# Early safe rows, later result loads, another order at the end of the attention and the choice in five units: attention and expert layers on one Trainium2 core

## What is computed

```
x = x + attn_a(layernorm(x))   # 16 heads, latent 32, rotary positions, causal softmax
x = x + ffn(layernorm(x))
x = x + attn_b(layernorm(x))   # 16 heads of 8, causal softmax
x = x + ffn(layernorm(x))

def ffn(flat):                 # 4096 x 128
    logits = flat @ gate_w + gate_b                  # 8 experts
    topv, topi = top_k(logits, 2); topw = softmax(topv)
    return sum over e of (gelu(flat @ w1[e] + b1[e]) @ w2[e] + b2[e]) * weight of e
```

## Time and profile before

| | us |
|---|---|
| median of three runs | 1233.25 |
| lowest and highest | 1228.84, 1236.98 |
| profiled execution, its own time | 1235.08 |
| its span | 1233.3 |
| mean granted TensorE clock | 0.918 |
| PE, DVE, ACT, POOL busy | 1038.6, 860.1, 656.8, 734.7 |

### The profile page before, as it was taken

One profiled execution on the slowest core, in us unless ns is written; L12 is line 12 of the kernel. 1 busy time (PEld: TensorE's weight loads), 2 busy tenths in 40 slices (PEclk: granted clock), 3 DMA queues, 4 the chain that ended last, 5 costly groups with the idle time before them and its releaser, 6 DMA issues.

```text
span 1233.3 us, 31859 instructions
## 1 busy us (share of the span) xinstructions
PE 1038.6 (84%) x11223; PEld 779.5 (63%) x11224; DVE 860.1 (70%) x2217; ACT 656.8 (53%) x1205; POOL 734.7 (60%) x809
## 2 busy tenths in 40 slices
PE   4689999988888988449988888999999974499995
PEld 3466666666665656239988745666666642398995
DVE  4697889888789997525565577677777764255665
ACT  1266776656465655115544556777777741154552
POOL 0476776767667777715544424667878866155553
PEclk9699999889699999769999989999999987599998
DMA  5340000000000000222333200000000002223335
GB/s 118 82 87 3 2 2 2 11 10 10 8 10 12 11 10 19 74 55 72 96 93 92 82 18 1 2 2 10 15 17 14 19 20 70 52 76 98 101 104 147
DMA packets 69358, 53.27 MB, mean 43 GB/s; under 512 B 20770, under 2 KB 61346, under 8 KB 69218
## 3 DMA queue, kind: packets, MB, share of 16 engines
q1 hardware_dynamic: 56578, 29.78, 9.6%
q0 software_dynamic: 9088, 18.70, 4.6%
q10 hardware_dynamic: 3552, 2.95, 1.0%
HBM read 27.57 MB, written 23.81 MB: 42 GB/s over the span
## 4 chain that ended last, share of the span: by engine, by line
PE 50%; DVE 25%; issue 8%; SPq 7%; DMA 4%; POOL 3%; ACT 2%; DVEq 0%; POOLq 0%; ACTq 0%
PE PS L1851 7%; PE PS L1533 5%; PE PS L1612 5%; PE PS L1663 4%; PE PS L1535 4%; PE PS L1534 4%; PE PS L1594 3%; DMA xg<-expert_in 3%; DVE M L1004 3%; DVE swapped L1032 2%; DVE M L996 2%; PE PS L1601 2%; SPq L582 2%; PE PS L1643 2%; DVE swapped L1030 2%
## 5 line engine op out<-in xcount | busy, mean ns | idle before, releaser
L1310 ACT ACTIVATE PT<-PS 128x768 f32<-128x768 f32 x256 | 206.7, 808 | 118.0 <-PE PS L1680 69.9
L754 POOL DMA_INDIRECT expert_out<-y_rows,dest x156 | 151.9, 974 | 194.8 <-DVE y_rows L1224 170.3
L643 POOL TENSOR_SCALAR_AFFINE_SELECT PT<-PT 128x512 f32<-128x512 f32 x256 | 185.7, 726 | 85.2 <-ACT PT L1310 84.4
L1446 ACT ACTIVATE hid<-PS,b_cols 128x256 f32<-128x256 f32 x312 | 122.2, 474 | 93.9 <-PE PS L1535 93.9
L1851 PE MATMUL PS<-W,hid 128*128 x1248 | 152.3, 275 | 0.2
L660 POOL DMA_INDIRECT expert_in<-rows,slots x128 | 130.0, 1015 | 29.6 <-issue 25.0
L1851 PEld LDWEIGHTS PS<-W,hid 128*128 128x128 f32 x1248 | 146.2, 192 | 0.5 <-issue 0.5
L1612 PE MATMUL PS<-PT,v_aug 128*32 128x256 f32 (+1 forms) x2048 | 115.1, 345 | 2.5 <-POOL PT L643 2.5
L1594 PE MATMUL PS<-causal_b,ident_b 128*128 128x256 bf16 x512 | 103.8, 287 | 8.2 <-DVE q_aug L1096 7.2
L1533 PE MATMUL PS<-xg_hi,w_hi 128*128 128x256 f32 x312 | 96.4, 309 | 2.3 <-DVE xg_lo L1203 1.7
L683 POOL TENSOR_TENSOR straight<-whole,C 128x512 f32<-128x512 f32 x64 | 82.8, 1293 | 21.0 <-ACT whole L1329 19.9
(11 more groups left out here) (292 smaller groups left out, 3159.9 us busy)
## 6 DMA issues: line engine op xcount, KB each, us to landing
xg<-expert_in SPq DMA_DIRECT2D x78, 129.0 KB
got<-expert_out SPq DMA_DIRECT2D x64, 128.0 KB
expert_out<-y_rows,dest POOLq DMA_INDIRECT x156
W<-in_L_ffn_w_dram SPq DMA_DIRECT2D x1, 2048.0 KB, 10.4
expert_in<-rows,slots POOLq DMA_INDIRECT x128
expert_in<-C SPq DMA_DIRECT2D x16, 128.0 KB
out_dram<-X SPq DMA_DIRECT2D x8, 256.0 KB
b_rows<-in_L_ffn_b_dram SPq DMA_DIRECT2D x2, 512.0 KB
```

What stands on the lines that cost most here:

```text
L643: nc.gpsimd.affine_select(out=diagonal, in_=diagonal, pattern=[[0, 4], [1, P]], compare_op=ALU.is_ge, fill=0.0, base=0, channel_multiplier ...
L754: nc.gpsimd.indirect_dma_start(out=expert_out, out_offset=bass.IndirectOffsetOnAxis(ap=dest[:, i % 4, b_:b_ + 1], axis=0), in_=y_rows[:, i ...
L1310: s.activation(PT[:, unit % 2, 2 * pair:2 * pair + 2, 0:3 * P], PS[:, 4:6, 0:3 * P], ACT.Exp).then_inc(m["exp_done"], 1)
L1446: ins = s.activation(hid[:, r % 2, k, :], h_bank[r % 2][k // 2][:, k % 2 * ROWS:(k % 2 + 1) * ROWS], ACT.Gelu, bias=b1_cols[:, bass.ds(e * ...
```

## The change

- `KNOWN` = 4 and `SAFE` = 3 x 512 + 256 = 1792. The ends are taken from the counts of chunk 4, as soon as its rank is done (in unit 1 of chunk 7's cycle in attention A, unit 0 in B), and 1792 rows behind each end are filled: up to 3 x 512 tokens may still come, and a tile may reach 256 rows further. The fills stand in SP's queue ahead of the wait for the attention's end; rows go out before numbers. The constant `aside` and `expert_out` grow with it.
- POOL waits for all fills before it sends chunk 5 (`send`, at k = 0), since the sends of chunks 5 to 7 overwrite safe rows.
- SP issues each result load one slot later than before; ACT waits for `attended` in place of `ends_ready`.
- `LAST`: out_t and out of chunk 7 come ahead of gate_t and gate of chunk 6; the statistics of chunk 7 use the other of two buffers, so that they don't meet those of chunk 6.
- In attention A POOL does the second `mask` of a unit in the next unit, behind `end_rope`, and the send behind `start_rope`.
- `PARTS_A`: the 13 parts of the choice stand in units 3 to 7, two, three, three, three and two of them, in place of units 4 to 7 with four, three, two and four.

```diff
+KNOWN = NCH - 4
+SAFE = (NCH - 1 - KNOWN) * CH + ROWS
...
-    put("aside", 2 * T + p[:, None] + P * np.arange((2 * E - 1) * RB))
+    put("aside", 2 * T + p[:, None] + P * np.arange((E * SAFE + SPARE) // P))
...
-    LAST = [("rank", 0, -2, 4), ("turn", 1, 0, 7), ("gate_t", 0, -1, 0), ("gate", 0, -1, 1), ("out_t", 0, 0, 2), ("out", 0, 0, 3), ("rank", 0, -1, 4),
+    LAST = [("rank", 0, -2, 4), ("turn", 1, 0, 7), ("out_t", 0, 0, 2), ("out", 0, 0, 3), ("gate_t", 0, -1, 0), ("gate", 0, -1, 1), ("rank", 0, -1, 4),
...
-PARTS_A = {4: range(0, 4), 5: range(4, 7), 6: range(7, 9), 7: range(9, 13)}
+PARTS_A = {3: range(0, 2), 4: range(2, 5), 5: range(5, 8), 6: range(8, 11), 7: range(11, 13)}
...
             for n, e_ in (("a", "1"), ("b", "2")):
                 me = moe_sems[e_]
-
-                sp.wait_ge(attended[n], 1)
-                sp.dma_start(b2_rows[:, :, :]...).then_inc(me["bias_ready"], 16)
 
                 sp.wait_ge(me["ends_ready"], 1)
                     for e in range(E):
-                        end = sp.value_load(end_of[0:1, e:e + 1], min_val=0, max_val=E * STRIDE - ROWS)
-                        sp.dma_start(expert_in[bass.ds(end, ROWS), D:WIDE].rearrange("(j p) w -> p j w", p=P),
-                                     con("aside")[:, e * RB:(e + 1) * RB].unsqueeze(2)).then_inc(me["filled"], 16)
-                        sp.dma_start(expert_in[bass.ds(end, ROWS), 0:D].rearrange("(j p) w -> p j w", p=P),
-                                     ident.unsqueeze(1).broadcast_to([P, RB, D])).then_inc(me["filled"], 16)
+                        end = sp.value_load(end_of[0:1, e:e + 1], min_val=0, max_val=E * STRIDE - SAFE)
+                        sp.dma_start(expert_in[bass.ds(end, SAFE), 0:D].rearrange("(j p) w -> p j w", p=P),
+                                     ident.unsqueeze(1).broadcast_to([P, SAFE // P, D])).then_inc(me["filled"], 16)
+                        sp.dma_start(expert_in[bass.ds(end, SAFE), D:WIDE].rearrange("(j p) w -> p j w", p=P),
+                                     con("aside")[:, e * SAFE // P:(e + 1) * SAFE // P].unsqueeze(2)).then_inc(me["filled"], 16)
+
+                sp.wait_ge(attended[n], 1)
+                sp.dma_start(b2_rows[:, :, :]...).then_inc(me["bias_ready"], 16)
...
                     load(i, r, least)
-                    if least >= LAG:
-                        load_results(i - LAG, (least - LAG) % CT, least - LAG)
+                    if least > LAG:
+                        load_results(i - LAG - 1, (least - LAG - 1) % CT, least - LAG - 1)
...
-                for tok in range(first_late, first_late + CT):
+                for tok in range(first_late - 1, first_late + CT):
...
                         pool.wait_ge(m["targets_ready"], c + 1)
+                        if c == KNOWN + 1:
+                            pool.wait_ge(moe_sems["1" if n == "a" else "2"]["filled"], 16 * 2 * E)
...
                     if unit and plan.project[unit - 1]:
                         end_rope(plan.project[unit - 1])
+                    if unit:
+                        mask(m, unit - 1, 1)
                     mask(m, unit, 0)
+                    if plan.project[unit]:
+                        start_rope(plan.project[unit])
                     if sends_at(unit, FIRST_SENT["a"]):
                         chunk, k = sends_at(unit, FIRST_SENT["a"])
                         send("a", chunk, range(k, k + 1))
-                    if plan.project[unit]:
-                        start_rope(plan.project[unit])
-                    mask(m, unit, 1)
...
+            def known_ends(m, me, s):
+                if s.c == KNOWN:
+                    dve.wait_ge(m["freed_dve"], s.freed)
+                    v.tensor_copy(end_of[:, :], counts[0:1, KNOWN, :]).then_inc(me["ends_ready"], 1)
...
-                own.did(v.tensor_copy(end_of[:, :], counts[0:1, NCH - 1, :]))
...
-                v.memset(scratch1[:, :], 0.0).then_inc(m["ends_ready"], 1)
...
-                act.wait_ge(m["ends_ready"], 1)
+                act.wait_ge(attended["a" if n == "1" else "b"], 1)
```

More of the change, by code:

```diff
@@ L42 @@
 _at = 0
-for _name, _n in (("ident", P), ("cos", S), ("sin", S), ("tile_no", TILES), ("ids", 2 * CT), ("aside", (2 * E - 1) * RB), ("first_row", E), ("prefer", E), ("steps", 6), ("place", 1),
+for _name, _n in (("ident", P), ("cos", S), ("sin", S), ("tile_no", TILES), ("ids", 2 * CT), ("aside", (E * SAFE + SPARE) // P), ("first_row", E), ("prefer", E), ("steps", 6), ("place", 1),
                   ("stack", 2), ("one24", 1),
@@ L215 @@
     FIRST_LATE = [("key", 2, 0), ("key", 3, 0), ("prep", 0, 1), ("key", 0, 1), ("key", 1, 1), ("key", 2, 1), ("key", 3, 1), ("prep", 0, 2)]
-    LAST = [("rank", 0, -2, 4), ("turn", 1, 0, 7), ("gate_t", 0, -1, 0), ("out_t", 0, 0, 1), ("gate", 0, -1, 2), ("out", 0, 0, 3), ("rank", 0, -1, 4),
+    LAST = [("rank", 0, -2, 4), ("turn", 1, 0, 7), ("out_t", 0, 0, 1), ("out", 0, 0, 3), ("gate_t", 0, -1, 0), ("gate", 0, -1, 2), ("rank", 0, -1, 4),
             ("gate_t", 0, 0, 7), ("gate", 0, 0, 0), ("rank", 0, 0, 1)]
@@ L332, in program @@
     expert_in = nc.dram_tensor("expert_in", [E * STRIDE + SPARE, WIDE], F32, kind="Internal").ap()
-    expert_out = nc.dram_tensor("expert_out", [2 * T + E * ROWS + SPARE, D], F32, kind="Internal").ap()
+    expert_out = nc.dram_tensor("expert_out", [2 * T + E * SAFE + SPARE, D], F32, kind="Internal").ap()
     result_tiles = expert_out[0:2 * T, :].rearrange("(t p k) d -> p t (k d)", p=P, k=2)
@@ L395, in program @@
         table_i = sb("table_i", [1, 5, TILES], I32)
+        end_of = sb("end_of", [1, E], I32)
         v_aug = sb("v_aug", [P, 2, CT, H, L])
@@ L457, in program @@
             table_f = sb("table_f", [P, 5], F32, moe)
-            end_of = sb("end_of", [1, E], I32, moe)
         used = [0, 0]
@@ L558, in _ @@
             with nc.allow_non_contiguous_dma(reason="one number in each row"):
-                sp.dma_start(expert_in[E * STRIDE:, D:WIDE].rearrange("(j p) w -> p j w", p=P), con("aside")[:, E * RB:].unsqueeze(2)).then_inc(spare_filled, 16)
+                sp.dma_start(expert_in[E * STRIDE:, D:WIDE].rearrange("(j p) w -> p j w", p=P), con("aside")[:, E * SAFE // P:].unsqueeze(2)).then_inc(spare_filled, 16)
                 sp.dma_start(expert_in[E * STRIDE:, 0:D].rearrange("(j p) w -> p j w", p=P), ident.unsqueeze(1).broadcast_to([P, SPARE // P, D])).then_inc(spare_filled, 16)
@@ L570, in _ @@
                     for e in range(E):
[L571 to L575 removed]
+                        end = sp.value_load(end_of[0:1, e:e + 1], min_val=0, max_val=E * STRIDE - SAFE)
[4 more added lines that the diff above has]
+                sp.wait_ge(attended[n], 1)
+                sp.dma_start(b2_rows[:, :, :].rearrange("p e d -> p (e d)"), b2.rearrange("e d -> (e d)").partition_broadcast(P)).then_inc(me["bias_ready"], 16)
                 sp.wait_ge(me["tiles_ready"], 1)
@@ L710, in attention_a @@
                         send("a", chunk, range(k, k + 1))
-                    if plan.project[unit]:
-                        start_rope(plan.project[unit])
-                    mask(m, unit, 1)
                     if statistics_a(unit) is not None:
                         root(m, normal_a(unit + 1)[1])
-                last_sends("a", m, 0)
+                mask(m, NCH * UNITS - 1, 1)
+                last_sends("a", m, 1)
             def attention_b():
@@ L744, in attention_b @@
                         root(m, *root_at(unit))
-                last_sends("b", m, 1)
+                last_sends("b", m, 0)
             def send_results(n):
@@ L1017, in close @@
                         dve.wait_ge(m["freed_dve"], s.freed)
-                        statistics(m, NCH - 1, 1 if n == "b" else 0)
+                        statistics(m, NCH - 1, 0 if n == "b" else 1)
                 dve.wait_ge(m["freed_dve"], plan.find("rank", 0, NCH - 1).freed)
@@ L1063, in attention_a @@
                         closing(m, w, plan.second[unit], True)
+                        known_ends(m, moe_sems["1"], plan.second[unit])
                     if unit + 1 < NCH * UNITS:
@@ L1130, in attention_b @@
                         closing(m, w, plan.rank[unit], False)
+                        known_ends(m, moe_sems["2"], plan.rank[unit])
                     summed = statistics_at(unit)
@@ L1376, in attention_a @@
                     if st.kind == "gate_t":
-                        normal("a", st.c, gate_norm_b(st.c), range(2, 4) if st.c < NCH - 1 else range(CT), gate=True)
+                        normal("a", st.c, gate_norm_b(st.c), range(2, 4) if st.c < NCH - 1 else range(CT), 0 if st.c < NCH - 1 else 1, gate=True)
                     step(st)
@@ L1422, in attention_b @@
                     if st.kind == "gate_t":
-                        normal("b", st.c, gate_norm_b(st.c), range(CT), 1, gate=True)
+                        normal("b", st.c, gate_norm_b(st.c), range(CT), 1 if st.c < NCH - 1 else 0, gate=True)
                     step(st)
```

1 line of the change is left out of this document (removed).

## The result

The changed kernel takes 1256.4 us (median of 4 runs, 1249.57 to 1266.05) against 1235.12 for the kernel before beside it. The ratio is 1.0195, 95% interval 1.0101 to 1.029: slower by 2%, clear of the noise, and outside my range of 1206 to 1254. Every ratio here compares fast runs alone, without those over 1.5% above the fastest of their kernel, so it can differ from the quotient of the medians. The profiled execution took 1249.57 us, span 1247.8, 14.5 more than before.

A forecast was written before the change was run, and what follows sets the result against it. Attention and expert tiles bound by work; idle before xg put down to the late fill. Early fill +6.5, PE's clock -1.5, choice and order -1 sum to +4.0 us on 1235.08: 1239.1, median about 1237, range 1206 to 1254.

The forecast's parts named there:

- p: Pace of one expert's pair of fill DMAs: 5.6 us for rows plus 1.1 for single numbers, 6.7 us together.
- the ends 4.15 and 8.8: Bounds on one expert's fill in us: 4.15 from the small fill's burst rate, 8.8 from the spare rows' landing at the start.
- 16p - 100.7: Change of both layers in us while POOL waits in both: +6.5 at 6.7 us per expert, break-even at 6.3.
- step from POOL's release to xg: From POOL's delayed start of chunk 5 to the first xg load: 31.85 us in both layers.
- the spare pair: Spare-row DMAs at the start, 1792 rows like the new fill; they land 8.8 us after their numbers are under way.
- POOL at chunk 5: POOL waits for the fill before chunk 5's sends, 14.4 us in layer 1, 22.8 in layer 2; root, gate, table follow.
- Room in layer 2: From chunk 4's counts to POOL's chunk 5 layer 2 has 34 us, layer 1 has 42; xg 6.7 us later.
- PE's clock, -1.5: At the first expert tiles PE would no longer start at about half clock: -1.5 us, bounds 0 and -4.6.
- Choice and POOL's order, -1, bounds -6 and +6: Choice in five units and POOL's new order in attention A shift DVE's collisions with POOL: -1 us, from -6 to +6.
- Result loads and last steps at 0: Result loads a slot later: 0, at best -2 us; out_t and out ahead of gate_t and gate: 0.
- Rival 2: POOL's wait at chunk 5 decides: 7.6 us per expert, waits of 21.6 and 30 us, median 1252; chance 0.26.
- both rivals: Rival 2, and rival 1: fill hidden at 4.15 us per expert, xg earlier in both layers, median 1204, chance 0.28.

The follow-up runs named there:

- the fill alone: Kernel before with only the early, larger fill and its wait at POOL; other edits left out: 1265.23 us, ratio 1.026.
- joined form: Changed kernel with each safe row and its number written as one piece of 516 bytes, same order of rows: 1223.23 us, ratio 0.9894 to the kernel before.
- all but the fill: Kernel before with every edit of the change except the fill, which stays late and small: 1227.23 us, ratio 0.9958.
- long rows: Changed kernel, rows and numbers joined, each partition writing eight or six adjacent rows in one piece up to 4128 bytes: 1200.79 us, 0.971; choice over four cycles 1196.1, 0.9719.
- the root first: Changed kernel with the root of chunk 7 ahead of chunk 5's sends on POOL: 1242.48 us, ratio 1.0047 to the kernel before.
- the order alone: Kernel before with only POOL's order in attention A changed (second mask put off a unit, rope ahead of send): 1228.05 us, ratio 0.9935.

## Why the prediction was wrong

The mechanism of the loss was right: POOL waits for the fill, and the root, the gate and the table slide behind it. The step that failed is the sizing of p, by the value that I took between the ends 4.15 and 8.8; the largest other miss is attention A, which I left almost unchanged and which got 14 us shorter by TensorE's clock. The equation, "the two layers change by 16p - 100.7 us as long as POOL waits in both", can be tried on the fill alone. There p is (516.04 - 450.73) / 8 = 8.2 in layer 1 and 8.0 in layer 2, and the equation gives +28; the two stretches from the last unit to xg are 13.0 and 16.9 us longer, +30, and the ratio 1.026 is +32. That it comes so near is in part luck: its step from POOL's release to xg is 9 us too short over both layers, and the fills started 3 and 4 us further ahead of the last unit than it had.

- **The pace p = 6.7 us: wrong.** Measured 8.0 and 7.9, mean 7.97; 16 x 1.27 = +20.3 us. The joined form shows which half failed. Rows alone were put at 5.6, and joined rows take 5.9. The 1792 single numbers I put at 1.1 us, from 1401 packets in one microsecond that held only 54 others; by that row itself 1792 of them take 1.3, and between streams of rows they cost 8.0 - 5.9 = 2.1. I had taken the quickest microsecond of the numbers beside the sustained rate of the rows, the very mistake that I warned of for the burst of the earlier trace rows. The landing of the spare pair, 8.8 us after its numbers were under way, held both in their true proportion and was nearer than my sum; I set its tail aside as paid once.
- **POOL at chunk 5, with the root, the gate and the table behind it: right.** Only the step from release to xg was short: 36.7 and 36.4 us instead of 31.85. Up to the start of the table's instructions on DVE it holds within 0.7 and 0.9 us. Then the table took 10.66 and 9.97 us instead of 7.26, and SP 3.25 and 3.51 instead of 2.55. Together +9.4. The slow table is not the wait's doing: it also comes in layer 2 of all but the fill (14.87) and of the long rows (11.38), and not in either layer with the root first (7.19, 7.05). Why DVE pauses between these small instructions stays open.
- **Room in layer 2:** chunk 4's counts now lie 26.3 us ahead of the last unit, 22.4 before: -4.
- **PE's clock, -1.5: wrong.** At the first tiles there is no gain: the granted clock is 0.58 from 545 to 550 as before, and 0.50 from 1080 to 1085 in layer 2. PE was busy 0.68 of the 5 us before 545: the way from table to the first rows stays longer than I had it, and PE stands idle again before it starts. Where the clock did move, in attention A, I had not looked.
- **Choice and POOL's order, -1, bounds -6 and +6: wrong.** Attention A is 9 to 19 us shorter in all ten profiles with the new order, and the order alone takes 0.65% (0.1 to 1.2) off the whole. The bounds came from DVE's collisions alone. What changed was PE's granted clock in the attention, 0.92 to 0.96, at the same idle time of PE; I had priced the clock only for the first tiles. By the Trainium skill (SBUF — State Buffer, SBUF: two separate sides) a DVE instruction with two SBUF inputs and a GpSimd one that reads SBUF hold each other up for a whole instruction. From that I had concluded that longer unbroken POOL work would cost DVE, the +6 side; the rope's product went from 926 to 737 and 814 ns instead. The long L976 of the earlier trace rows agree with the rule; my conclusion from it did not hold.
- **Result loads and last steps at 0: right in this neighbourhood,** 1.001 alone. With the long rows, where POOL waits for no fill, they are worth about 0.9%.

Summed with the measured sizes: 4.0 + 20.3 + 9.4 - 4 + 1.5 - 13.2 (attention A) - 2 (start) + 1.3 (attention B) - 3.1 (experts) = +14.2, and the profile shows +14.5. That is bookkeeping between the same two profiles and tests nothing. The experts' part is unexplained: the first experts take 169 to 171 us in the five kernels without the later result loads, and with them 161 to 164 in five, but 168, 171 and 171 in three others and 183 with the root first. Rival 2 had the right story (1252 at p = 7.6) and I gave it 0.26; two errors of opposite sign that it shares with my forecast, the step to xg (+9.4) and attention A (-13.2), then kept the result near it by luck.

The unnamed way out of both rivals was the shape of the packets. The best kernels of this study, long rows with the choice in five or four cycles, are at 0.971 and 0.9719 of the kernel before, faster than either; their intervals do not tell them apart.

## What to carry to other kernels

Before a transfer is moved ahead and made larger, price it at what it sustains in its final shape, with all its pieces in the mix that they will run in, and multiply by its repeats: an error of 1.3 us in one pair became 20 us. If the price is high, change the shape before the place: one piece per partition of rows that lie together moved nearly three times the bytes per microsecond of a row and a number apart (355 and 126 GB/s over the whole fill). And when an in-order engine gets a new wait, list what stands behind it by consumer; here two chains did, and of the 54 us that freeing one of them won up to xg, 41 were lost again in the experts. And before a shorter stretch is put down to fewer waits, compare the engine's idle time, its busy time and its granted clock: here the idle time had not moved.

## What the hardware showed that I had not expected

- The shape of the pieces set the rate at full DMA engines: 126, 172 and 355 GB/s over a whole fill for 4 and 512 bytes, 516 bytes, and up to 4128 bytes.
- The fill at 355 GB/s is not seen to slow the attention: attention A takes 420.0 us with it, 418.7 with the slow fill, and 413.8 to 423.7 over all kernels with the new order of POOL's work.
- SP's own queue was held by the slow fill: one of its DMAs took up to 5.59 us to issue, where the long form's took at most 0.99. Line L571 of the changed kernel (issue in ns, min, median, max):

```profile
L571 SPq DMA_DIRECT2D expert_in<-C x16: 393/3900/5593, 437.1 to 1025.0; - x16
```

- Taking 11 us of stalls away from DVE, an engine that is busy 70% of the span, gained nothing. Reordering POOL's work left PE's idle time in attention A where it was and shortened it by 9 to 19 us, because TensorE was granted 0.94 to 0.96 of its clock there instead of 0.92 to 0.93.
